# A Mamba-2 block and a feed-forward block on one core: eight whole blocks of 512 tokens in place of seven whole and two half ones, with new instruction orders

## The reference

```python
x = x + layernorm(mamba2(layernorm(x)))        # sequential in time, within a sequence
x = x + layernorm(ffn(layernorm(x)))           # token by token

def mamba2(u):
    z, xBC, dt = split(u @ in_proj)            # 256 -> 512 + 768 + 8
    xBC = silu(causal_conv(xBC, taps=4))       # x (8 heads x 64), B (128), C (128)
    dt = softplus(dt + dt_bias); dA = dt * -exp(A_log)
    # by chunks: Y = (C B^T * exp(segsum(dA))) (x dt)  +  C state * exp(cumsum(dA))
    #            state = state * exp(sum(dA)) + B^T (x dt * decay)
    y = (Y + D * x) * silu(z)
    return rmsnorm(y) @ out_proj

def ffn(x):                                    # Wg, Wu, Wd = table[code] * scale
    return (gelu_tanh(x @ Wg.T) * (x @ Wu.T)) @ Wd.T
```

## Time and profile before

| | |
|---|---|
| median of 3 runs | 960.33 us (960.23 to 961.1) |
| profiled execution, its own time | 961.48 us |
| its span in the trace | 959.8 us |
| busy share of the span | PE 93%, PEld 81%, DVE 78%, ACT 64%, POOL 37% |
| busy | PE 889.1, DVE 752.7, ACT 618.5, POOL 355.3 us |
| matmuls | 6400 |
| granted TensorE clock, mean | 0.984 |

### The profile page before, as it was taken

The page is one execution under the profiler, slowest core; times in us unless marked ns, Lnnn a source line. Parts: engine busy times, 40 slices in busy tenths (PEclk is TensorE's granted clock), DMA queues, the critical chain, the costliest instruction groups (busy, mean ns, idle before and its releaser), DMA issues.

```text
span 959.8 us, 17690 instructions
## 1 busy us (share of the span) xinstructions
PE 889.1 (93%) x6400; PEld 776.2 (81%) x6400; DVE 752.7 (78%) x2031; ACT 618.5 (64%) x1034; POOL 355.3 (37%) x342
## 2 busy tenths in 40 slices
PE   4388889999999999999999999999999999999987
PEld 3368687889897888888898898988888898888886
DVE  5988999787888697887888788787978888786232
ACT  5857887857759385765858395774858485673222
POOL 2031526253343525253342616243442525244323
PEclk9589999999999999999999999999999999999999
DMA  7501010201002010200102010110102010010000
GB/s 224 183 1 56 1 57 2 67 1 44 14 12 67 1 56 1 78 1 14 45 13 66 2 56 1 45 34 13 45 13 67 1 56 2 23 45 2 1 23 12
DMA packets 19206, 34.59 MB, mean 36 GB/s; under 512 B 2480, under 2 KB 11440, under 8 KB 19120
## 3 DMA queue, kind: packets, MB, share of 16 engines
q1 hardware_dynamic: 18256, 33.44, 11.1%
q10 hardware_dynamic: 864, 0.03, 0.1%
HBM read 29.14 MB, written 4.33 MB: 35 GB/s over the span
## 4 chain that ended last, share of the span: by engine, by line
PE 62%; DVE 16%; ACT 11%; issue 5%; POOL 3%; DMA 1%; SPq 0%; POOLq 0%; DVEq 0%; ACTq 0%
PE fb L1083 27%; PE db L1083 14%; PE mb L1083 10%; DVE xc L891 3%; PE mb L1199 3%; PE mb L1190 3%; ACT L711 2%; POOL hl L589 2%; ACT hid L711 2%; PE mb L1180 1%; ACT xc L671 1%; PE mb L1205 1%; ACT xc L664 1%; DVE st L1008 1%; ACT L671 1%
## 5 line engine op out<-in xcount | busy, mean ns | idle before, releaser
L589 POOL TENSOR_TENSOR hl<-hid,hl 128x512 fp32r<-128x512 f32 (+1 forms) x144 | 183.8, 1281 | 344.5 <-ACT hl L718 344.3
L1083 PE MATMUL fb<-x1t,wg 128*128 128x512 f32 (+1 forms) x864 | 213.5, 382 | 5.6 <-DVE x1t L994 2.9
L1083 PE MATMUL db<-wd,hl 128*128 128x256 f32 x1536 | 217.6, 291 | 0.7 <-POOL hl L589 0.7
L1083 PE MATMUL fb<-x1t,wu 128*128 128x512 f32 (+1 forms) x864 | 202.7, 370 | 13.4 <-ACT hid L711 13.3
L1083 PEld LDWEIGHTS db<-wd,hl 128*128 128x128 f32 x1536 | 195.7, 191 | 15.2 <-issue 10.5
L1083 PEld LDWEIGHTS fb<-x1t,wu 128*128 128x128 f32 x864 | 149.8, 189 | 48.9 <-ACT hid L711 22.7
L1083 PEld LDWEIGHTS fb<-x1t,wg 128*128 128x128 f32 x864 | 146.1, 189 | 37.4 <-issue 10.1
L711 ACT ACTIVATE hid<-fb 128x512 f32<-128x512 f32 (+1 forms) x144 | 78.4, 550 | 129.8 <-PE fb L1083 115.5
L891 DVE SCALAR_TENSOR_TENSOR xc<-raw,cw,xc 128x256 f32<-128x256 f32 x288 | 135.7, 539 | 5.3 <-ACT xc L664 3.2
L1000 DVE TENSOR_TENSOR hid<-fb,hid 128x512 f32<-128x512 f32 (+1 forms) x144 | 90.0, 626 | 58.9 <-PE fb L1083 34.2
L559 POOL TENSOR_TENSOR rs<-ve,neg_half 128x1 f32<-128x1 f32 (+2 forms) x89 | 62.0, 697 | 168.0 <-DVE ve L793 62.5
(11 more groups left out here) (143 smaller groups left out, 1319.8 us busy)
## 6 DMA issues: line engine op xcount, KB each, us to landing
lmat<-rows SPq DMA_DIRECT2D x32, 512.0 KB, 4.4
xin<-in_u SPq DMA_DIRECT2D x16, 256.0 KB, 2.7
out<-xb SPq DMA_DIRECT2D x16, 256.0 KB, 2.2
wg_raw<-in_packed SPq DMA_DIRECT2D x4, 256.0 KB, 13.2
wg_raw<-in_scales SPq DMA_DIRECT2D x4, 256.0 KB
wu_raw<-in_packed SPq DMA_DIRECT2D x4, 256.0 KB, 12.3
wu_raw<-in_scales SPq DMA_DIRECT2D x4, 256.0 KB
wd_raw<-in_packed SPq DMA_DIRECT2D x4, 256.0 KB, 13.2
```

The lines of the kernel that those rows point to most:

```text
L589: pool.tensor_tensor(hl[:, hs, n % 2, 1, :], hid[:, hs, n % 2, :], hl[:, hs, n % 2, 0, :].bitcast(F32), ALU.subtract).then_inc(s["lo"], 1)
L1083: last = pe.matmul(ps, lhs(a, k), rhs(b, k), start=start and n == 0, stop=stop and n == len(todo) - 1, skip_group_check=check)
```

## The change

The blocks are moved by half a block, so that they fall together with halves of sequences: eight whole blocks, two for each sequence. The last FFN, which has nothing beside it, then covers 512 tokens, and so does the first Mamba. All tables are new. `SUMS_ON_ACT` now names the two halves of block 0, which is one half fewer on ACT.

```diff
-NBLK = BATCH * SEQ // BLK + 1
+NBLK = BATCH * SEQ // BLK
...
-        wi_split:0 wi_z:0 xn_split:1 rates:0 dq:0 taps:3 dq:1 silu:3 dl:0 dq:2 taps:4 dq:3 dq:4 dt_bias:1 gate:3
+        wi_split:0 wi_z:0 rates:0 dq:0 xn_split:0 dq:1 dq:2 taps:0 dq:3 dq:4 gate:0 dq:5 gate:1 wo_split:0 dq:6
...
-SUMS_ON_ACT = ((0, 1), (1, 0), (1, 1))
+SUMS_ON_ACT = ((0, 0), (0, 1))
...
 def there(name, k, i):
 
-    if not isinstance(i, int):
-        return True
-    if name in PER_HALF and (i, k // PER_HALF[name]) in ((0, 0), (NBLK - 1, 1)):
-        return False
     return 0 <= i < NBLK
...
 def tiles(f):
 
-    if isinstance(f, int) and f in (0, NBLK - 1):
-        return range(TT // 2, TT) if f == 0 else range(TT // 2)
     return range(TT)
...
-            absent = 0 if name in whole else per_block[name] // 2
-            return i * per_block[name] - absent + (k + 1)
+            return i * per_block[name] + (k + 1)
...
-            run(LAST[engine], NBLK, 1)
+            run(LAST[engine], NBLK, NBLK % 2)
...
-                src = u_v[bass.ds(i * 2 + (j - 1), 1)].rearrange("o p c d -> (o p) c d")
+                src = u_v[bass.ds(i * 2 + j, 1)].rearrange("o p c d -> (o p) c d")
...
-                if par == 0 and k < 3:
+                if par == 1 and k >= 3:
 
                     last = dve.memset(hist[:, pair, :], 0.0)
...
-                if par == 0 and q == 1:
+                if par == 1 and q == 3:
 
                     dve.memset(state[:], 0.0).then_inc(s["state"], 1)
```

More of the change, by code:

```diff
@@ L98 @@
+        xdt:3 split:12< stats2:2 yoff:3 split:13< split:14< ln2:2 stats2:3 split:15< ln2:3 fin:0<""",
 }
@@ L1116, in ip @@
                 last.then_inc(s["ip"], 1)
-            def warm(i, par, k):
-                if k == 0:
-                    pe.wait_ge(consts_ready, 1)
-                for n in range(2):
-                    pe.matmul(db[0][:, CH * n:CH * n + CH], ident[:], upto[:], start=True, stop=True)
             def cs(i, par, j):
@@ L1246, in dn, with warm @@
                 last.then_inc(s["down"], 1)
+            def warm(i, par, k):
+                if k == 0:
+                    pe.wait_ge(consts_ready, 1)
+                for n in range(2):
+                    pe.matmul(db[0][:, CH * n:CH * n + CH], ident[:], upto[:], start=True, stop=True)
             drive(pe, "pe", dict(xt=xt, ip=ip, cs=cs, ct=ct, z=z, gb=gb_, xtr=xtr, yo=yo, yd=yd, st=st, yt=yt_, out=out_,
```

161 lines of the change are left out of this document (83 added, 78 removed).

## The result

| | before | after |
|---|---|---|
| median, us | 960.34 (959.51 to 961.25, 10 runs) | 964.2 (961.5 to 968.58, 10 runs) |
| profiled execution, its own time | 961.48 | 964.03 |
| its span | 959.8 | 962.3 |
| granted TensorE clock, mean | 0.984 | 0.975 |

The ratio of the means is 1.0045, with an interval of 1.0027 to 1.0064: slower, but by 0.45% (the medians lie 3.9 us apart) and not by the predicted 1.2%. 964.2 lies inside the stated range (956 to 982) and barely inside the forecast's own one (963.5 to 980).

What follows compares the result with a forecast made beforehand. Iterations were taken as TensorE-bound, the opening as bound by DVE and the serial Mamba chain. Opening 241 plus 730 (five iterations 546.5, last 106, end 77.5) gave span 971, median 971.5 us; range 956 to 982, own range 963.5 to 980.

Steps and rivals of the forecast that it cites:

- the blocks' price: Whole kernel: whole blocks make the opening longer and the rest 53.3 us shorter, about 1.2% slower in all.
- the sum: Whole kernel: iterations start at 241 us, plus 730 behind that, gives 971 us of span.
- the opening: Everything up to the second gu:0: was 176.5 us, predicted 241, 11 us behind the even point.
- the last iteration: The iteration without a next block: 109.3 less 7.7 of PE work plus 4.5 of waiting, 106 us.
- the last part: The whole FFN alone at the end: 68.5 us, then 9.0 to the end of the span, 77.5 in all.
- the 124: Opening's first part: predicted start of the first gu:0 in us, 7 ahead of the first inter at 131.
- the second part: Opening between first and second gu:0: DVE paces up to inter:7 at 184, then 57 us more, to 241.
- Rival 1: Opening costs no more than DVE's work: iterations start at 223.5, time 954 us; chance 0.14.
- 5 x 109.3 = 546.5: The five equal iterations: each still takes the 109.3 us of the kernel before.
- Rival 2: Iterations lose their gelu waits through 18 table loads in place of 21: 9.5 us less, 962; chance 0.08.
- the 4.5: Before the last gu:0: PE idle, in us, for the uncovered layer norm, transpose and split chain.
- Rival 3: Iterations: PE waits 1.5 us five times at yd:0 for the HBM round trip, opening late too: 986; chance 0.12.

Runs made afterwards that it cites:

- e2: The changed kernel (eight whole blocks, its FIRST and LAST) with the ORDER table of the kernel before; 976.57 us, ratio 1.0168.
- e1: The kernel before (nine blocks, its own FIRST and LAST) with only the ORDER table of the changed kernel; 952.6 us, ratio 0.9923.
- e11: e1 with two pairs of extra function-table switches per iteration where ACT is idle (22 loads), later buffers keeping their offset modulo 512; 952.78 us, ratio 0.9918.
- e15: The kernel before with split:1, split:10 and silu:2 moved earlier on ACT and cs:0 ahead of gu:0 on PE; 973.53 us, ratio 1.0136.

## Why the prediction was right or wrong

**The direction and the blocks' price: right, the price 3.3 us too low.** The prediction's story of the whole blocks (slower opening, part of it given back behind it) is what `e2` measured at the old iteration. Its span is 974.3 us, where the sum said 971: 0.9 more in the opening, 0.8 in the last iteration, 1.5 in the last part. The median is +16.1 us, where the sum said +11 (971.5 - 960.3); the other 1.7 us are the runs around the profiled one, whose median lies 2.2 us over the span in place of 0.5.

**The opening: right, partly by luck.** The steps at the start, to be laid beside the earlier trace rows: ACT's `xnt`, then DVE's `wi`, PE's first product and `ip:1`, and SP's store of `csr`.

```profile
14.40 0.60 ACT L621 ACTIVATE xnt<-mb 128x512 fp32r<-128x512 f32 x1
...
17.95 1.75 DVE L757 TENSOR_TENSOR wi<-wi_raw,wi 128x1536 fp32r<-128x1536 f32 x1
...
19.84 3.01 PE L1082 MATMUL mb<-wi,xnt 128*128 128x264 f32 x12 [5.48 <-DVE wi L760]
30.20 2.90 PE L1082 MATMUL mb<-xnt,wi 128*128 128x256 f32 x12 [5.45 <-ACT sz L678]
...
39.36 0.35 SPq L485 DMA_DIRECT2D rows<-csr  x1
```

PE starts at 19.84 (21 was said) and `csr` is stored at 39.4 (42.5). The first `sums` is then not at 53 but at 49.55, and the first `inter` at 129.75 (131):

```profile
49.55 0.17 DVE L850 COPY ct_<-mb 128x16 f32<-128x16 f32 x1
...
129.75 0.69 DVE L999 TENSOR_TENSOR hid<-fb,hid 128x512 f32<-128x512 f32 x1
```

DVE's windows up to the one and from there to the other:

```profile
0.00:49.55 49.55, 16.82 (x88) 15.40 (x89) 32.34 (x85) 30.38 (x47) 5.56 (x15) 0.84 0.63 197
49.55:129.75 80.20, 60.35 (x458) 50.21 (x457) 68.61 (x183) 49.94 (x105) 19.23 (x21) 0.88 0.07 22
```

So DVE had 101.0 us of work (101.7 was said), 17.2 of idle time before `sums` (19.5) and 11.6 behind it (10). The luck is in the last step: `gu:0` leads `inter` by 4.7 us and not by 7, which makes up for the 1.25 us by which `inter` came too early, and leaves the 124 only 1.0 off. In the second part `inter:7` came at 184.2 (184), and `gu:0` at 243.15.

A step that was missed is that the change also puts POOL's `wi_split` ahead of `stats1:0`, so that PE's first transposes wait until 13.28 and end at 14.36; ACT's queue, which the prediction did see, is free at 14.27, so the two delays of `xnt` come out alike. The 2.96 us of `wi` were 1.75, for which see the last section. Rival 1 (the opening costs no more than DVE's work, 223.5) is refuted by 243.15.

**The iteration: wrong, and this is the step that failed.** "5 x 109.3 = 546.5" took the old iteration for the new one. The sum thus holds the 1.9 us of waits for `gelu` as a constant, on the argument that the new order only moves the places where `gelu` stands behind other work. It was never checked on the places themselves, although both the order and the trace were there: how long before the up product of `gu:n+1` does `gelu:n` end? In the kernel before it is 0.05 us at n = 0, 3 and 12, the least that any place shows, and PE is idle there for 0.4, 0.6 and 0.8 us. In `e1` and in the changed kernel it is 0.05 at n = 1 alone, where PE is idle for 0.01 us at most (the up product begins 1.54 us after its gate product, where 1.36 is the rule), and 0.3 or more everywhere else. An iteration has 109.3 - 107.3 = 2.0 us without PE, so a whole new set of tables could take up to 2.0 x 5 = 10 us off the sum, and that bound belonged into the range with more than 0.08. The measured iteration has 107.1 us of PE's work and 0.5 without, and five of them took 537.47 us, 9.0 less than the term. Rival 2 had this outcome and its price, 9.5 us less and 962; that the kernel took 964.2 has other grounds (+2.15 in the opening, -2.9 and +1.1 behind, and a median 0.2 us over the profiled run in place of 1.15 under it). Its reason was wrong, though: 22 loads run as fast as 18 (`e11`).

**The last iteration: the same error once more.** Of the 2.9 us by which it is shorter than the term 1.9 are the waits for `gelu` again: `e2` has them in this iteration too. Most of the rest is the wait for `x1t` ahead of the last `gu:0`, in PE's timeline:

```profile
878.82 1.70 PE L1082 MATMUL db<-wd,hl 128*128 128x256 f32 x12 [0.69 <-POOL hl L588]
881.07 0.66 PE L1214 MATMUL fb<-ident,x1n 128*128 128x128 f32 x4 [0.55 <-DVE x1n L988]
883.71 2.68 PE L1082 MATMUL fb<-x1t,wg 128*128 128x512 f32 x6 [1.98 <-DVE x1t L993]
```

It is 2.0 us, with 0.7 and 0.5 ahead of it, so 3.2 where 4.5 were said. With the old order `e2` has 2.58 for `x1t` and 2.08 for `x1n`, 4.7 in all, so the 4.5 was right for the old tables. The new DVE table takes `x1_split:0` ahead of `fin`, which the term did not follow; that this step makes the difference is argued and not tested.

**The last part: right but for one wait.** 78.59 against 77.5. From the last product to the end:

```profile
950.10 3.15 PE L1082 MATMUL db<-wd,hl 128*128 128x256 f32 x24 [0.70 <-POOL hl L588]
```

It ends at 953.25, so 9.05 us of layer norm and stores follow (9.0 was said), and the FFN takes 69.5 in place of 68.5. It holds this wait of 0.7, and behind the wait for `x1t` above a stretch at the lower clock: granted 0.50 from 884 to 886, and the first two groups of six matmuls take 2.5 and 1.9 us to the next in place of 1.4, 1.7 us lost. The half FFN of before has no such stretch behind its wait of 2.73 us.

**Rival 3** (`yd:0` waits for the round trip) is refuted for the iterations: PE's only wait in one is 0.3 us for `sz`.

## What to carry to other kernels

When a change brings new tables along with its named edit, price the tables as an edit of their own, bounded by all the idle time of the bounding engine in the repeated part, and times the number of repeats; here that term, 9 us, was larger than the 3.9 us of the whole result. A wait of the bounding engine is a distance between two steps, so take it from both orders at each place, not from the count of costly instructions. And a tight schedule is hard to take over in pieces: of eight trials that moved two to seven steps, or the last fifth, from a better order into a worse one, seven made it slower. In `e15` the step had a partner on another engine that had stayed behind; for the others the cause was not isolated.
